# Ratio attention of a perceiver block: where GpSimd's value spread, key spread and bias addition stand against the tile's exponentials

## The chip, the cores and the metric

The kernel runs on one core of a Trainium2 chip. The time is the device time of one execution in microseconds; the kernel before has a median of 784.0 us over three runs, from 782.09 to 784.91. Smaller is better.

## The reference

Two layers run over x, 32 batches of 32 tokens with 256 features, each token's part added to x: a cross attention with a distance bias over 257 context rows, the **ratio attention**, a quantised feed-forward net, a second cross attention, a long and a segment attention, and a mixture of experts. The change touches the ratio attention alone:

```
qkv = layernorm(x) @ w_qkv + b_qkv;  q, k, v in 16 heads of 16
dot = q . k
vals = |q|^2 + |k|^2
scores = dot * dot / (vals - 2 dot + 1e-6) + causal mask (-1e9)
out = softmax(scores) @ v @ w_out + b_out;  x = x + out
```

## The kernel before, in words

The 1024 tokens are 8 tiles of 128 tokens (4 batches of 32). Five engines have instruction streams of their own and meet at semaphores only. The cross attention runs first, about to 260 us of the span, then the ratio attention to about 358 us, then the rest.

In the ratio attention each engine runs one step function per slot u, and one slot handles several tiles at different depths. The steps u = -2 (or -3) to 6 are in the block of the cross attention; what is left of tile 7 runs in the next block, after a barrier of all engines. The work of one tile n, in the order of its data:

- **Norm**: VectorE takes statistics (`norm_stats`, L1158 to L1163), GpSimd the inverse root (`root`, L1013 to L1015), VectorE applies it (`norm_apply`, L1169) in slot n - 4.
- **Projection**: TensorE turns the tile (L848), ScalarE copies it (L1074), TensorE projects queries and keys (L856), ScalarE evicts them (L1085 to L1093).
- **Key spread**: GpSimd multiplies the keys by head masks into `kbd` (helper `spread_heads`, L872, two instructions, slot n - 2). ScalarE squares `kbd` (L1078). TensorE forms numerator and denominator (helper `per_batch`, L896, slot n - 1).
- **Scores**: ScalarE evicts the denominator (L1102) and the squared numerator (L1104), VectorE takes the reciprocal (L1225), GpSimd multiplies (L1045) and adds the causal mask (L1048).
- **Softmax**, slot n: VectorE takes the row maximum (L1187) and subtracts it (L1188), ScalarE takes the exponentials (L1065, semaphore `p_ready`), VectorE turns blocks (helper `turn_blocks`, L933).
- **Values**: ScalarE copies the projected values (L1108), GpSimd spreads them by batch into `vbd` (helper `spread_batches`, L879, slot n). TensorE weighs them (helper `weigh_values`, L923). ScalarE takes sums and own heads (L1055, L1058), VectorE normalises and turns them (L1174, L1175, L956), TensorE projects (L865), VectorE adds the result to x (L1205). That last addition needs the output bias row in x already: GpSimd adds it (L1039, semaphore `bias_added`), in slot n - 2.

GpSimd's step u of the kernel before, in its queue's order: root of tile u+4, value spread of u, key spread of u+2, bias addition of u+2, multiplication and mask of u+1. VectorE's step u: statistics of u+4, normalising and turning of u-1, output addition of u-2, maximum and subtraction of u, `norm_apply` of u+4, block turning of u, reciprocal of u+1. The order is written out by hand in the step functions; nothing schedules it otherwise.

Of the kernel before, what the change touches and what calls it, by code (L numbers as in the profile page):

```python
# [21 lines left out]
ALU = mybir.AluOpType  # L22
# [44 lines left out]
def at_least(eng, sem, value):  # L67

    if isinstance(value, int) and value <= 0:
        return  # L70
    eng.wait_ge(sem, value)
# [797 lines left out]
def spread_heads(eng, kbd, kT, head):  # L869

    src = kT[:].rearrange("p (b k) -> p b k", b=BT)
    return eng.tensor_tensor(kbd, src.unsqueeze(2).broadcast_to([P, BT, 4, SQ]),  # L872
                             head.unsqueeze(1).unsqueeze(3).broadcast_to([P, BT, 4, SQ]), ALU.mult)


def spread_batches(eng, vbd, v, c):

    each = [P, 2 * NG, 2, 32]
    return eng.tensor_tensor(vbd[:, :, :, 0:32], v[:].rearrange("p (n d) -> p n d", d=32).unsqueeze(2).broadcast_to(each),  # L879
                             c.pair.unsqueeze(1).unsqueeze(3).broadcast_to(each), ALU.mult)  # L880
# [93 lines left out]
def there(u, count=NT):  # L974
    return not isinstance(u, int) or 0 <= u < count


class RatioAttention:


    def __init__(self, nc, sb, sem, psum, bank, c, x, w, loaded):
# [3 lines left out]
        bq2, wide, row = sb("bq2", [P, KT]), sb("wide", [P, KT, P]), sb("row", [P, D])  # L985
# [13 lines left out]
        consts_set, marked, row_full, row_ready = sem("consts_set"), sem("marked"), sem("row_full"), sem("row_ready")  # L999
        var_ready, rstd_ready, xn_ready = sem("var_ready"), sem("rstd_ready"), sem("xn_ready")  # L1000
# [5 lines left out]
        sub_ready, p_ready, pT_ready = sem("sub_ready"), sem("p_ready"), sem("pT_ready")  # L1006
        o_full, o_read, o_ready, oT_ready = sem("o_full"), sem("o_read"), sem("o_ready"), sem("oT_ready")
        y_full, y_done, bias_added = sem("y_full"), sem("y_done"), sem("bias_added")
# [4 lines left out]
        def root(pool, n):  # L1013
            pool.wait_ge(var_ready, n + 1)
            nc.gpsimd.tensor_tensor(rstd[n % 2][:], veps[n % 2][:], c.half[:, 0:1], ALU.pow).then_inc(rstd_ready, 1)  # L1015
# [5 lines left out]
            pool.wait_ge(marked, 2)  # L1021

        def pool_step(pool, u):
            if there(u + 4):
                root(pool, u + 4)
            if there(u):
                pool.wait_ge(v_done, u + 1)
                at_least(pool, o_full, u - 1)
                spread_batches(nc.gpsimd, vbd[u % 2], v, c).then_inc(vbd_ready, 1)
            if there(u + 2):  # L1030
                n = u + 2
                pool.wait_ge(k_ready, n + 1)
                at_least(pool, s_full, n - 1)
                for m in range(KT):
                    ins = spread_heads(nc.gpsimd, kbd[n % 2][:, m, :, :, :], kT[:, m, :], c.head)
                ins.then_inc(kbd_ready, 1)
                pool.wait_ge(xn_ready, n + 1)
                pool.wait_ge(row_ready, 1)
                nc.gpsimd.tensor_tensor(x[:, n, :], x[:, n, :], row[:], ALU.add).then_inc(bias_added, 1)  # L1039
            if there(u + 1):  # L1040
                n = u + 1
                pool.wait_ge(s_read, n + 1)
                pool.wait_ge(inverse_ready, n + 1)
                at_least(pool, p_ready, n - 1)
                nc.gpsimd.tensor_tensor(num[n % 2][:], square[n % 2][:], inverse[n % 2][:], ALU.mult) \  # L1045
                    .then_inc(ratio_ready, 1)
                pool.wait_ge(ratio_ready, n + 1)
                nc.gpsimd.tensor_tensor(num[n % 2][:], num[n % 2][:],  # L1048
                                        c.causal.unsqueeze(1).broadcast_to([P, NH, SQ]), ALU.add) \
                    .then_inc(masked_ready, 1)  # L1050

        def act_own(act, n):
            act.wait_ge(o_full, n + 1)
            at_least(act, o_ready, n)
            nc.scalar.copy(sums[:].rearrange("p (i b) -> p i b", b=BT), shares(o_banks)[:, :, :, 32])  # L1055
            for h in range(4):
                mine, at = slice(SQ * h, SQ * h + SQ), DH * (h % 2)
                ins = nc.scalar.copy(o_own[mine, :].rearrange("p (b i d) -> p i b d", b=BT, i=NG),  # L1058
                                     shares(o_banks)[mine, :, :, at:at + DH])
            ins.then_inc(o_read, 1)  # L1060
# [166 lines left out]
        self.root, self.norm_stats, self.norm_apply = root, norm_stats, norm_apply  # L1227
        self.pool_start, self.pe_start, self.dve_start, self.dve_row = pool_start, pe_start, dve_start, dve_row
        self.pool, self.act, self.pe, self.dve = pool_step, act_step, pe_step, dve_step
        self.act_own, self.act_exp, self.pe_output, self.pe_values = act_own, act_exp, pe_output, pe_values  # L1230
        self.dve_features, self.dve_output = features, dve_output
# [1703 lines left out]
```

## Time and profile before

| what | value |
|---|---|
| median of three runs | 784.0 us (782.09 to 784.91) |
| the profiled execution | 782.49 us, its span 780.7 us |
| TensorE busy | 659.7 us (84%), mean granted clock 0.938 |
| VectorE busy | 496.9 us (64%) |
| ScalarE busy | 359.7 us (46%) |
| GpSimd busy | 311.6 us (40%) |

The span is the time from the first to the last instruction seen by the profiler; 1.79 us of the execution lie around it. The shares are means over all stages. In the rows below PE is TensorE, PEld its weight load, DVE VectorE, ACT ScalarE, POOL GpSimd. PEclk is the granted clock as a share of 2.4 GHz. In the timeline a row is: start us, duration us, engine, line, operation, out<-in, count, and in brackets the idle time before it and what ended it. An instruction's duration includes time in which it has been issued and can't proceed. Buffer numbers are left out, and `late`, `shared` are regions in which the tiles of the ratio attention lie.

### The profile page before, as it was taken

To read this page: it belongs to the slowest core of one execution; us is meant where nothing else is said; L and a number is where in the kernel's file an instruction comes from. 1 tells how busy PE (TensorE), PEld (TensorE's weight loads), DVE (VectorE), ACT (ScalarE), POOL (GpSimd) and SP (SyncE) were. 2 spreads that over 40 slices of the span, in tenths; PEclk is the share of its full clock that TensorE was granted. 3 is DMA by queue.
4 is the path that set the end of the run, shared out by engine and by line. 5 is a ranking of instruction groups with operands and counts; after the bars stand their busy time and mean duration, and the time that the engine had idled before them with its cause. 6 is when DMAs were issued, how large, how long until landed. Compare 5 with 4: busy or idle time off the path is not lost. (4 is left out here: it accounts for less than half of the span.)

```text
span 780.7 us, 16875 instructions
## 1 busy us (share of the span) xinstructions
PE 659.7 (84%) x6081; PEld 502.5 (64%) x6081; DVE 496.9 (64%) x1365; ACT 359.7 (46%) x976; POOL 311.6 (40%) x445
## 2 busy tenths in 40 slices
PE   4999999999999877744993699978998884999990
PEld 3768777877877766643441587657776662677770
DVE  3677776776776789857368873556886786333330
ACT  1445454545545566734375753434655541223220
POOL 2244545555552377731000020233745533455641
PEclk9999999999999999976997799998999996999996
DMA  9632323222220000007500134609101021234334
GB/s 276 218 75 62 78 60 78 76 66 72 65 55 2 2 3 3 3 1 229 230 2 0 68 155 170 258 3 406 68 3 61 2 83 54 42 65 67 60 47 67
DMA packets 31697, 65.08 MB, mean 83 GB/s; under 512 B 5792, under 2 KB 21792, under 8 KB 29312
## 3 DMA queue, kind: packets, MB, share of 16 engines
q1 hardware_dynamic: 26016, 55.73, 21.7%
q0 software_dynamic: 4688, 7.18, 5.8%
q10 hardware_dynamic: 912, 1.10, 0.5%
q8 instruction: 50, 0.82, 0.4%
q14 instruction: 31, 0.25, 0.1%
HBM read 57.67 MB, written 7.37 MB: 83 GB/s over the span
## 5 line engine op out<-in xcount | busy, mean ns | idle before, releaser
L487 ACT ACTIVATE prob<-s_sb,negm 128x257 f32<-128x257 f32 x128 | 66.2, 517 | 94.2 <-DVE negm L710 94.2
L424 POOL TENSOR_SCALAR bias<-dist,cst 128x257 f32<-128x257 f32 x128 | 59.8, 486 | 97.8 <-DVE dist L697 88.0
L706 DVE CUSTOM_DVE_ANT_0 s_sb<-psum,bias 128x257 f32<-128x257 f32 x128 | 49.4, 423 | 51.5 <-PE psum L567 48.2
L545 PE MATMUL psum<-ctxT,shared 128*128 128x257 f32 x256 | 62.9, 389 | 1.7 <-DMA msk<-in_mask 1.7
L553 PE MATMUL psum<-shared,ctxT 128*128 128x256 f32 x256 | 60.4, 379 | 0.0
L2616 PE MATMUL psum<-ex_w,shared 128*128 x184 | 58.3, 460 | 0.6 <-ACT shared L2509 0.6
L1706 POOL TENSOR_TENSOR wn<-wn,cst 128x1 f32<-128x1 f32 x8 | 4.7, 588 | 123.9 <-DVE wn L1833 123.9
L553 PEld LDWEIGHTS psum<-shared,ctxT 128*128 128x128 f32 x256 | 48.4, 189 | 6.8
L545 PEld LDWEIGHTS psum<-ctxT,shared 128*128 128x128 f32 x256 | 47.2, 195 | 8.0 <-issue 2.4
L567 PE MATMUL psum<-kT,qbd 64*128 64x257 f32 x256 | 48.6, 429 | 2.7 <-DVE mx L706 2.5
L2616 PEld LDWEIGHTS psum<-ex_w,shared 128*128 128x128 f32 x184 | 33.1, 190 | 15.4 <-issue 0.8
L2800 DVE TENSOR_TENSOR shared<-psum,shared 128x352 f32<-128x352 f32 x23 | 12.1, 524 | 48.4 <-ACT shared L2525 48.4
L1445 PE MATMUL psum<-shared,ff_used_up 128*128 128x512 f32 x96 | 41.6, 593 | 0.0
L872 POOL TENSOR_TENSOR shared<-shared,cst 128x512 f32<-128x512 f32 x32 | 34.5, 1099 | 14.9 <-ACT shared L2038 14.9
L592 PE MATMUL psum<-pT,v 128*64 128x128 f32 x512 | 35.0, 279 | 2.8 <-DVE o_keys L759 2.8
L592 PEld LDWEIGHTS psum<-pT,v 128*64 128x64 f32 x512 | 27.4, 136 | 13.2 <-issue 13.1
L2525 ACT ACTIVATE shared<-psum 128x352 f32<-128x352 f32 x23 | 10.7, 464 | 52.8 <-PE psum L2616 52.8
L578 PE MATMUL psum<-cst,prob 128*128 128x128 f32 x256 | 35.0, 279 | 0.0
L2626 PE MATMUL psum<-ex_w,shared 128*128 x138 | 33.7, 380 | 0.8 <-DVE shared L2791 0.8
L567 PEld LDWEIGHTS psum<-kT,qbd 64*128 64x128 f32 x256 | 22.5, 184 | 18.4 <-DVE mx L706 10.0
L856 PE MATMUL psum<-shared,late 128*128 128x128 f32 x256 | 34.3, 290 | 0.0
L578 PEld LDWEIGHTS psum<-cst,prob 128*128 128x128 f32 x256 | 27.4, 141 | 10.5 <-issue 10.5
(349 smaller groups left out, 1656.5 us busy)
## 6 DMA issues: line engine op xcount, KB each, us to landing
ctxT<-in_ctx_T SPq DMA_DIRECT2D x32, 257.0 KB
ex_w<-in_w SPq DMA_DIRECT2D x1, 5632.0 KB, 17.3
kpos<-in_kpos SPq DMA_DIRECT2D x32, 128.5 KB
msk<-in_mask SPq DMA_DIRECT2D x32, 128.5 KB
near_turned<-in_ctx_T_tiles SPq DMA_DIRECT2D x4, 1028.0 KB
ff_used_up<-in_ctx_T_tiles SPq DMA_DIRECT2D x4, 1028.0 KB
near_rows<-in_ctx_tiles SPq DMA_DIRECT2D x4, 1024.0 KB, 7.5
ff_used_up<-in_ctx_tiles SPq DMA_DIRECT2D x4, 1024.0 KB, 7.2
```

Source lines behind the costliest of these rows:

```text
L424: nc.gpsimd.tensor_scalar(bias[n % 2][:, g, :], dist[n % 2][:], c.slope[:, g:g + 1], 1.0, ALU.mult, ALU.mult).then_inc(bias_ready, 1)
L487: nc.scalar.activation(prob[n % 2][:, g, :], s_sb[n % 2][:, g, :], ACT.Exp, bias=negm[:, b, g:g + 1], accum_out=esum[t % 2][:, b, g:g + 1]) \
L545: ins = nc.tensor.matmul(kv[m][:, 0:SK], w["xa_k"][:, k, P * m:P * m + P], ctxT[n % BT][:, k, :], start=(k == 0), stop=(k == KT - 1))
L553: ins = nc.tensor.matmul(kv[0][:, D * i:D * i + D], ctxT[n % BT][:, k, P * i:P * i + P], w["xa_v"][:, k, :], start=(i == 0 and k == 0), st ...
L567: nc.tensor.matmul(sc[g % 2][:, 0:SK], qbd[t % 2][lo:lo + 64, g // 2, b, :, :].rearrange("p h q -> p (h q)"), kT[n % 2][lo:lo + 64, g // 2 ...
L578: ins = nc.tensor.transpose(pt[j][:, at:at + P], prob[n % 2][:, g, P * i:P * i + P], c.ident)
L592: ins = nc.tensor.matmul(oo[64 * half:64 * half + 64, at:at + P], v[n % BT][:, i, 64 * g:64 * g + 64], pT[n % 2][:, g, i, :], start=(n % 2 ...
L706: nc.vector.tensor_tensor_reduce(s_sb[n % 2][:, g, :], sc[g % 2][:, 0:SK], bias[n % 2][:, g, :], 1.0, float("-inf"), ALU.add, ALU.max, mx[ ...
L856: ins = nc.tensor.matmul(dst[:, P * m:P * m + P], weight[:, k, P * m:P * m + P], xT[:, k, :], start=(m == 0 and k == 0), stop=True, skip_g ...
L872: return eng.tensor_tensor(kbd, src.unsqueeze(2).broadcast_to([P, BT, 4, SQ]), head.unsqueeze(1).unsqueeze(3).broadcast_to([P, BT, 4, SQ]) ...
L1445: ins = nc.tensor.matmul(bank[2 + n % 6][:], wt[:, k, P * m:P * m + P], xT[:, k, 512 * h:512 * h + 512], start=(k == 0), stop=(k == KT - 1))
L2616: ins = nc.tensor.matmul(y_bank[part][:, 0:FE], rT[j % 2][:, k, :], ex.w1[:, bass.ds(e, 1), k, FE * part:FE * part + FE].rearrange("p a f ...
```

## The change

In GpSimd's step the bias addition is moved ahead of the value spread and gets one wait more: for the exponentials of tile u, where u is 0 or more. As the queue is in order, value spread and key spread stand behind that wait too. The root moves from the head of step u (tile u+4) to the end of step u (tile u+5), and the first root, of tile 2, is called at the head of step -2. Nothing else changes: the operations, their number and their operands are the same.

```diff
         def pool_step(pool, u):
-            if there(u + 4):
-                root(pool, u + 4)
+            if u == -2:
+                root(pool, 2)
+            if there(u + 2):
+                n = u + 2
+                pool.wait_ge(xn_ready, n + 1)
+                pool.wait_ge(row_ready, 1)
+                at_least(pool, p_ready, u + 1)
+                nc.gpsimd.tensor_tensor(x[:, n, :], x[:, n, :], row[:], ALU.add).then_inc(bias_added, 1)
             if there(u):
                 pool.wait_ge(v_done, u + 1)
                 at_least(pool, o_full, u - 1)
@@ -1034,9 +1040,6 @@
                 for m in range(KT):
                     ins = spread_heads(nc.gpsimd, kbd[n % 2][:, m, :, :, :], kT[:, m, :], c.head)
                 ins.then_inc(kbd_ready, 1)
-                pool.wait_ge(xn_ready, n + 1)
-                pool.wait_ge(row_ready, 1)
-                nc.gpsimd.tensor_tensor(x[:, n, :], x[:, n, :], row[:], ALU.add).then_inc(bias_added, 1)
             if there(u + 1):
                 n = u + 1
                 pool.wait_ge(s_read, n + 1)
@@ -1048,6 +1051,8 @@
                 nc.gpsimd.tensor_tensor(num[n % 2][:], num[n % 2][:],
                                         c.causal.unsqueeze(1).broadcast_to([P, NH, SQ]), ALU.add) \
                     .then_inc(masked_ready, 1)
+            if there(u + 5):
+                root(pool, u + 5)
```

`at_least` issues no wait for a value of zero or less, and `there(n)` is true for tiles 0 to 7.

## Rows read from the trace of the kernel before

**Rows 1.** Page, busy time by engine: us, share of the span, instructions.
```profile
PE 659.7 (84%) x6081; PEld 502.5 (64%) x6081; DVE 496.9 (64%) x1365; ACT 359.7 (46%) x976; POOL 311.6 (40%) x445
```

**Rows 2.** Windows, the slot of tile 2: length, busy PE, PEld, DVE, ACT, POOL, PEclk, DMA.
```profile
296.50:306.30 9.80, 6.92 (x175) 6.18 (x181) 9.23 (x13) 6.47 (x17) 7.23 (x8) 0.83 0.00 0
```

**Rows 3.** Timeline, VectorE, tile 2's maximum up to tile 3's.
```profile
296.50 0.69 DVE L1187 TENSOR_REDUCE shared<-late 128x16 f32<-128x512 f32 x1 [0.37 <-POOL late L1048]
297.22 1.31 DVE L1188 TENSOR_TENSOR late<-late,shared 128x512 f32<-128x512 f32 x1
298.45 1.13 DVE L1169 TENSOR_SCALAR shared<-x,shared 128x256 f32<-128x256 f32 x1
299.50 0.70 DVE L933 STREAM_TRANSPOSE late<-late 128x512 f32<-128x512 f32 x1
300.13 3.30 DVE L1225 RECIPROCAL late<-late 128x512 f32<-128x512 f32 x1
...
304.32 0.79 DVE L1175 TENSOR_TENSOR shared<-shared 128x256 f32<-128x256 f32 x1
...
306.29 0.69 DVE L1187 TENSOR_REDUCE shared<-late 128x16 f32<-128x512 f32 x1 [0.39 <-POOL late L1048]
```

**Rows 4.** Timeline, GpSimd, the same slot.
```profile
296.43 0.55 POOL L1015 TENSOR_TENSOR shared<-shared,cst 128x1 f32<-128x1 f32 x1
296.94 1.04 POOL L879 TENSOR_TENSOR shared<-shared,cst 128x512 f32<-128x512 f32 x1
297.94 2.54 POOL L872 TENSOR_TENSOR late<-shared,cst 128x512 f32<-128x512 f32 x2
300.44 0.63 POOL L1039 TENSOR_TENSOR x<-x,shared 128x256 f32<-128x256 f32 x1
303.56 1.27 POOL L1045 TENSOR_TENSOR late<-late 128x512 f32<-128x512 f32 x1 [2.50 <-issue]
304.91 1.35 POOL L1048 TENSOR_TENSOR late<-late,cst 128x512 f32<-128x512 f32 x1
```

**Rows 5.** Timeline, GpSimd, the key spread of tile 0, before the slots.
```profile
263.88 2.04 POOL L872 TENSOR_TENSOR late<-shared,cst 128x512 f32<-128x512 f32 x2 [3.31 <-ACT shared L1085]
```

**Rows 6.** Timeline, VectorE, tile 4's slot, and tile 7's subtraction after it.
```profile
316.09 0.69 DVE L1187 TENSOR_REDUCE shared<-late 128x16 f32<-128x512 f32 x1 [0.37 <-POOL late L1048]
316.81 0.79 DVE L1188 TENSOR_TENSOR late<-late,shared 128x512 f32<-128x512 f32 x1
318.30 0.71 DVE L933 STREAM_TRANSPOSE late<-late 128x512 f32<-128x512 f32 x1 [0.70 <-ACT late L1065]
...
325.10 0.69 DVE L1187 TENSOR_REDUCE shared<-late 128x16 f32<-128x512 f32 x1 [0.37 <-POOL late L1048]
...
348.18 0.69 DVE L1188 TENSOR_TENSOR late<-late,shared 128x512 f32<-128x512 f32 x1
```

**Rows 7.** Source view of `norm_apply`: ns min/median/max, first and last start us.
```profile
L1169 DVE TENSOR_SCALAR shared<-x,shared x8: 415/1126/1129, 234.6 to 308.2; 128x256 f32<-128x256 f32 x8
```

**Rows 8.** Timeline, ScalarE: value copy, own heads, and tile 4's exponentials.
```profile
300.15 0.37 ACT L1108 COPY shared<-psum 128x256 f32<-128x256 f32 x1
...
301.09 1.50 ACT L1058 COPY shared<-psum 32x256 f32<-32x256 f32 x4
...
317.64 0.63 ACT L1065 ACTIVATE late<-late 128x512 f32<-128x512 f32 x1 [2.36 <-DVE late L1188]
```

**Rows 9.** Timeline, TensorE: tile 2's slot, and two rows of tile 7's scores.
```profile
300.25 0.70 PE L923 MATMUL psum<-shared,late 64*64 64x66 f32 x32 [2.88 <-DVE late L933]
...
301.16 3.12 PE L856 MATMUL psum<-shared 128*128 128x128 f32 x16
...
305.97 0.70 PE L896 MATMUL psum<-shared,cst 64*32 64x128 f32 x32
...
328.70 1.75 PE L896 MATMUL psum<-late,shared 64*32 64x128 f32 x64
...
331.54 1.06 PE L896 MATMUL psum<-shared,cst 64*32 64x128 f32 x32 [0.24 <-ACT shared L1078]
```

## The prediction

> **What bounds the kernel now.** The page first: TensorE is busy 84% of the span and GpSimd 40% [rows 1]. That is a mean over stages and says nothing of this one. The windows by slot show another picture: in tile 2's slot of 9.80 us VectorE is busy 9.23, GpSimd 7.23 and TensorE 6.92 us, although TensorE's granted clock is 0.83 there [rows 2]. So the timelines of VectorE and GpSimd decide. A slot runs from one tile's row maximum to the next's. In tile 2's slot VectorE goes maximum 296.50, subtraction 297.22, `norm_apply` 298.45, block turning 299.50, reciprocal 300.13 [rows 3]; GpSimd goes on with the multiplication at 303.56 and the mask at 304.91, and the next maximum starts at 306.29 [rows 3, 4]. It is one loop through two engines with no gap: 9.79 us. Four slots have this form, of tiles 0 to 3; from tile 4 on there is no `norm_apply` left and a slot is 325.10 - 316.09 = 9.01 us [rows 6].
>
> Two instructions in that loop are longer than their work. The subtraction takes 1.31 us [rows 3], and 0.69 when GpSimd is idle [rows 6]. `norm_apply` takes 1.13 us, and its shortest record is 0.415 [rows 3, 7]. GpSimd's rows say why: the value spread ends at 297.98, and the subtraction, issued at 297.22, ends 0.55 us after that; `norm_apply`, issued at 298.45, ends at 299.58, after the first of the two key spreads, which are 2.54 us together here and 2.04 where nothing collides [rows 4, 5]. Whichever of the two engines comes second stands until the other's instruction is over. In tile 4's slot, with no root ahead of it, the value spread comes earlier and the subtraction needs 0.79 [rows 6].
>
> The Trainium skill has this rule, on the page "SBUF — State Buffer", section "SBUF: two separate sides": GpSimd and VectorE share a port pair that is held for a whole instruction, and VectorE wants it with two SBUF inputs or in a two-port mode. The trace agrees for the subtraction, at 1.31 against 0.69 us. Was the reciprocal to want the pair too, the change would lose: the bias addition would stand until the reciprocal is over, and the slot would come to some 12 us. Rows exclude it: the bias addition ran at 300.44 for 0.63 us inside the reciprocal of 300.13 to 303.43, and the second key spread lay beside the block turning, which took 0.70 us, as against 0.71 in tile 4's slot [rows 3, 4, 6].
>
> **The change, part by part.** It adds and removes no instruction but the wait.
>
> *Root.* In the queue's cyclic order it stays between the mask of one tile and the spreads of the next; called at the end of a step, it is only kept ahead of the new wait. It runs from 0.07 us ahead of the maximum to 0.48 behind its start [rows 3, 4], and the subtraction starts at +0.72: no collision. Cost 0.
>
> *Wait for the exponentials.* It stands in the steps of tiles 0 to 5; in tile 6's the bias addition, and the wait with it, doesn't exist, so that slot stays as it is. Let 0 be the start of the maximum. The subtraction starts at +0.72 and now takes 0.69 us. In tile 4's slot the exponentials start at +1.55 [rows 6, 8] with 0.10 us of collision in it (0.79 less 0.69), so they start at +1.45 and end at +2.08. `norm_apply` runs behind the subtraction from about +1.34 to +1.75, beside the exponentials and with GpSimd idle: hidden, with 0.3 us to spare. Block turning: +2.21 in tile 4's slot [rows 6], less 0.10: +2.11. It was +3.00 [rows 3]. From there on the loop is as it was: 0.63 to the reciprocal, 3.43 to the multiplication (+6.17), 1.35 to the mask, 1.38 to the next maximum: 8.90 us. So 4 slots give 0.89 us each, 3.56, and tiles 4 and 5 give 0.10 each, 0.20. Sum 3.76 us.
>
> *What is queued behind the wait.* GpSimd starts at +2.15 (0.07 behind the exponentials) with 0.63 for the bias, 1.04 for the value spread and 2.04 for the key spread [rows 4, 5]: 3.71, so it is done at +5.86, and the multiplication is wanted at +6.17. Cover 0.31 us. Beside it VectorE only turns blocks and takes the reciprocal, which do not collide (above). If the key spread stayed at 2.54, GpSimd would be 0.19 late in 6 slots and give back 1.1 us.
>
> *Who waits for the spreads.* The value spread of the tile now ends at +3.82 instead of +1.48. The weighing of values on TensorE starts at +3.75 now [rows 3, 9] and would start at +3.9. ScalarE's copy of the next tile's values, at +3.65 now [rows 8], waits for the same spread, so it goes to about +3.85 and ends at +4.2; the own heads behind it start 0.84 us after the weighing [rows 8, 9], at +4.7, and end at +6.2. VectorE wants them only after its reciprocal at +6.05, ahead of a normalisation that must stand for the multiplication anyway (0.79 us at 304.32 [rows 3]). Hidden. TensorE: after the values at 300.25 the last part of the scores ended at 306.67, 6.42 us later, with the slow clock in between [rows 9]; from +3.9 that is +10.3. Those scores are evicted behind the next exponentials, at 8.90 + 2.0 = +10.9. Cover 0.6 us in a slot like this. The key spread, at +5.86, is ahead of the squares (after the own heads, at +6.5) and of the scores. So all of it costs 0, and what is late next is TensorE.
>
> *Before and after the slots.* In step -2 the bias addition moves into idle time (3.31 us ahead of the first key spread [rows 5]); in step -1 it delays a key spread by 0.63 us, which no loop needs then. After tile 6 a barrier follows GpSimd's last mask; all behind it, loads included, is released by semaphores of this stage and moves up as a whole. 0.
>
> The sum against the profiled execution: 782.49 - 3.76 = 778.7 us. That execution lies 1.5 us under the median of 784.0, so on the median's footing it is 780.2, a ratio of 0.9952. About 0.3%, or 2.35 us, is what a measurement of this kernel can tell from no change.
>
> **The rivals.**
>
> *Less of the gain.* The wait is longer than the 0.07 us I take from ScalarE to GpSimd, or the spreads take their collided length. Each 0.1 us beyond the cover of 0.31 costs 0.6 us. With 0.5 us late in each of 6 slots, 3.0 of 3.76 are given back: 783.2. For: it is a cover of 0.3 us in a loop with three engines. Against: every duration in it is from a row. Chance 0.13.
>
> *TensorE becomes the bound* (the other side). Its granted clock falls to 1.2 GHz in some slots: the projection takes 3.12 us in tile 2's slot, and tile 7's scores, slow throughout, ran from 328.70 to 332.60, 3.9 us, against 2.4 here (from the end of the projection, 304.28, to 306.67) [rows 9]. Slow throughout, the scores would end 0.91 + 3.12 + 3.9 = 7.9 us after the values began, at +11.8 or later with the turning slow too (+12.1). It decides once they end behind +10.9. A slot would be 8.90 + 1.2 = 10.1 us, six of them 60.6 against 57.2 now (4 of 9.79 and 2 of 9.01): 3.4 slower, 787.4. For: the values begin no earlier in a slot that is shorter. Against: the slow stretches cover part of a slot only (0.83 in the mean [rows 2]), and shorter slots leave TensorE less idle time. Chance 0.05.
>
> The skill's page "TensorE: Matmul & The Clock Gate", section "What's actually happening", ties the clock to how busy the array has been lately; by it the shorter slots speak against this rival. No row here shows a slot of 8.9 us.
>
> *No change to speak of.* The stage gets shorter, but what follows takes it back: a barrier, a load or a slow clock behind the ratio attention that doesn't move with it. Nothing there waits for an absolute time. 784.0. Chance 0.10.
>
> **How the numbers follow.** Forecast 0.72, the rivals 0.13, 0.05 and 0.10. The predicted time is the likeliest's, 780.2. The range: the runs of before spread from 1.9 under to 0.9 over their median; a luckier clock takes it to 778.0, and upward it takes in the smaller gains and stops at 783.8 (about 0.1 lies above, 0.08 below). Faster by over 0.3%: 0.72 less the part that noise hides plus the milder half of the first rival, 0.71; same 0.23; slower 0.06.
>
> **What would show it right or wrong.** Right: subtraction at 0.69, `norm_apply` at 0.42, the key spread pair at 2.04 us; slots of 8.9 us for tiles 0 to 5; GpSimd idle ahead of the bias addition, released by L1065, and 0.3 us idle ahead of the multiplication. Wrong: a multiplication with no idle time ahead of it (GpSimd late), an eviction at L1102 that waits for L896 (TensorE), a subtraction still over 1 us (the collision was not with the spreads), or a block turning that waits for anything but the exponentials.

## The result, and the profile after

| | before | changed |
|---|---|---|
| median of 12 runs | 783.56 us (781.96 to 785.27) | 780.39 us (778.25 to 782.14) |
| profiled execution | 782.49 us, span 780.7 | 778.49 us, span 776.7 |
| mean granted clock of TensorE | 0.938 | 0.940 |
| VectorE busy | 496.9 us | 490.4 us |
| GpSimd busy | 311.6 us | 309.6 us |

The ratio is 0.996, with a 95% interval of 0.9946 to 0.9974: 3.1 us gained, between 2.0 and 4.2. The changed kernel is faster by 0.4%, beyond the 0.3% that can be told from no change, though the interval's near end, 0.26%, is just inside it. The lines of the helpers (L872, L879, L896, L923, L933, L956) keep their numbers; `norm_apply` is L1174 now (was L1169), the maximum L1192 (L1187), the subtraction L1193 (L1188), the reciprocal L1230 (L1225), the normalisation L1180 (L1175), the bias addition L1031 (L1039), multiplication and mask L1048 and L1051 (L1045, L1048), the exponentials L1070 (L1065), the value copy L1113 (L1108).

First the timeline of VectorE in the changed kernel, tile 2's slot and then tile 4's, as in [rows 3] and [rows 6]:

```profile
294.92 0.69 DVE L1192 TENSOR_REDUCE shared<-late 128x16 f32<-128x512 f32 x1 [0.39 <-POOL late L1051]
295.64 0.69 DVE L1193 TENSOR_TENSOR late<-late,shared 128x512 f32<-128x512 f32 x1
296.25 0.41 DVE L1174 TENSOR_SCALAR shared<-x,shared 128x256 f32<-128x256 f32 x1
297.02 0.71 DVE L933 STREAM_TRANSPOSE late<-late 128x512 f32<-128x512 f32 x1 [0.37 <-ACT late L1070]
297.66 3.31 DVE L1230 RECIPROCAL late<-late 128x512 f32<-128x512 f32 x1
...
303.85 0.69 DVE L1192 TENSOR_REDUCE shared<-late 128x16 f32<-128x512 f32 x1 [0.39 <-POOL late L1051]
...
312.75 0.69 DVE L1192 TENSOR_REDUCE shared<-late 128x16 f32<-128x512 f32 x1 [0.38 <-POOL late L1051]
313.47 0.69 DVE L1193 TENSOR_TENSOR late<-late,shared 128x512 f32<-128x512 f32 x1
...
321.67 0.69 DVE L1192 TENSOR_REDUCE shared<-late 128x16 f32<-128x512 f32 x1 [0.38 <-POOL late L1051]
```

The subtraction is down from 1.31 to 0.69 us, `norm_apply` from 1.13 to 0.41. The block turning starts 2.10 us after the maximum (3.00 before) and stands 0.37 us for the exponentials: the chain through ScalarE is now what VectorE waits for there. Tile 2's slot takes 303.85 - 294.92 = 8.93 us, tile 4's 8.92.

GpSimd in the same slot, as in [rows 4]:

```profile
294.84 0.55 POOL L1015 TENSOR_TENSOR shared<-shared,cst 128x1 f32<-128x1 f32 x1
297.16 0.64 POOL L1031 TENSOR_TENSOR x<-x,shared 128x256 f32<-128x256 f32 x1 [1.77 <-ACT late L1070]
297.75 1.04 POOL L879 TENSOR_TENSOR shared<-shared,cst 128x512 f32<-128x512 f32 x1
298.75 2.04 POOL L872 TENSOR_TENSOR late<-shared,cst 128x512 f32<-128x512 f32 x2
301.10 1.28 POOL L1048 TENSOR_TENSOR late<-late 128x512 f32<-128x512 f32 x1 [0.31 <-issue]
302.46 1.35 POOL L1051 TENSOR_TENSOR late<-late,cst 128x512 f32<-128x512 f32 x1
```

It idles for 1.77 us while the subtraction and `norm_apply` run, then does its three jobs at full speed (the key spread pair takes 2.04 us, not 2.54), and is done 0.31 us before the multiplication. Before the change the idle time stood ahead of the multiplication, 2.50 us in one piece [rows 4].

Where the 4.0 us of the two profiled spans went: tile 0's maximum starts at 277.06 (276.90 before) and tile 6's at 330.60 (334.10), so the six slots between them take 53.54 us instead of 57.20: **3.66 us less**. Behind them the first matmul of the feed-forward net (L1445, now L1450) starts at 366.4 instead of 370.1, and the first of the experts (L2616, now L2621) at 659.0 instead of 662.9. What was won in the stage is carried to the end.

### The profile page after: what moved, and what is told of

It is laid out like the page before. It is cut to its first block and busy times, and to the rows that moved or that the text cites. A ratio compares the mean times of both kernels' runs of the same rounds, so it can differ in the third digit from the quotient of the medians.

```text
span 776.7 us, 16875 instructions
## 1 busy us (share of the span) xinstructions
PE 656.7 (85%) x6081; PEld 501.0 (64%) x6081; DVE 490.4 (63%) x1365; ACT 360.6 (46%) x976; POOL 309.6 (40%) x445
## 5 line engine op out<-in xcount | busy, mean ns | idle before, releaser
L2621 PE MATMUL psum<-ex_w,shared 128*128 x184 | 58.3, 460 | 0.6 <-ACT shared L2514 0.6
L2621 PEld LDWEIGHTS psum<-ex_w,shared 128*128 128x128 f32 x184 | 33.1, 190 | 15.4 <-issue 0.8
L1450 PE MATMUL psum<-shared,ff_used_up 128*128 128x512 f32 x96 | 41.6, 593 | 0.0
L872 POOL TENSOR_TENSOR shared<-shared,cst 128x512 f32<-128x512 f32 x32 | 34.5, 1100 | 14.9 <-ACT shared L2043 14.9
```

The costliest lines, as they stand in the source:

```text
L1450: ins = nc.tensor.matmul(bank[2 + n % 6][:], wt[:, k, P * m:P * m + P], xT[:, k, 512 * h:512 * h + 512], start=(k == 0), stop=(k == KT - 1))
L2621: ins = nc.tensor.matmul(y_bank[part][:, 0:FE], rT[j % 2][:, k, :], ex.w1[:, bass.ds(e, 1), k, FE * part:FE * part + FE].rearrange("p a f ...
```

## The experiments

Three questions: is it the collision on the port, or the order of GpSimd's queue, that gave the gain; how much room does GpSimd have behind the wait; and what would use the idle time better. The port theory is that of the prediction. Its rival, the order theory, is that the bias addition no longer stands last ahead of the multiplication, and that this shortens the slot. The first four kernels ran on one chip and the last four on another, each beside the kernel before, so kernels of the two groups are compared by their ratios to it. Slots are read from the starts of the maxima. An edit moves the line numbers behind it by a few lines.

**The changed kernel again.** No edit.

> The changed kernel once more, as the mate of the others on this chip. Expected 3.2 to 3.8 us under the kernel before, ratio about 0.9955: slots of tiles 0 to 5 at 8.92 us, subtraction 0.69, norm_apply 0.41, key spread pair 2.04.

780.77 us, ratio 0.9959 (0.9946 to 0.9972). The slots of tiles 0 to 5 take 53.54 us again, 276.89 to 330.43.

**Without the wait.**

```diff
                 pool.wait_ge(row_ready, 1)
-                at_least(pool, p_ready, u + 1)
                 nc.gpsimd.tensor_tensor(x[:, n, :], x[:, n, :], row[:], ALU.add).then_inc(bias_added, 1)
```

> The changed order (bias addition first, root at the end) without the wait for the exponentials. Port theory: the bias addition runs from +0.48 to +1.1 after the maximum's start, the subtraction stands for it and ends at about +1.7, the value spread follows and norm_apply stands for it; block turning at about +3.0 as in the kernel before, slots of tiles 0 to 3 at 9.7 to 9.9 us, time 783.5, ratio 0.999 to 1.002. Order theory (the gain comes from the bias addition no longer standing last, ahead of the multiplication, and the wait adds nothing): slots of 8.9 us, ratio about 0.996.

784.06 us, ratio 1.0004 (0.9991 to 1.0018): nothing is left of the gain. The timelines of VectorE (tile 2's slot, then tile 4's) and of GpSimd beside them:

```profile
295.53 0.69 DVE L1191 TENSOR_REDUCE shared<-late 128x16 f32<-128x512 f32 x1 [0.38 <-POOL late L1050]
296.25 0.90 DVE L1192 TENSOR_TENSOR late<-late,shared 128x512 f32<-128x512 f32 x1
297.08 1.12 DVE L1173 TENSOR_SCALAR shared<-x,shared 128x256 f32<-128x256 f32 x1
298.13 0.70 DVE L933 STREAM_TRANSPOSE late<-late 128x512 f32<-128x512 f32 x1
...
304.92 0.69 DVE L1191 TENSOR_REDUCE shared<-late 128x16 f32<-128x512 f32 x1 [0.37 <-POOL late L1050]
...
315.06 1.38 DVE L1192 TENSOR_TENSOR late<-late,shared 128x512 f32<-128x512 f32 x1
```

```profile
295.98 0.63 POOL L1030 TENSOR_TENSOR x<-x,shared 128x256 f32<-128x256 f32 x1
296.57 1.49 POOL L879 TENSOR_TENSOR shared<-shared,cst 128x512 f32<-128x512 f32 x1
...
314.84 1.05 POOL L879 TENSOR_TENSOR shared<-shared,cst 128x512 f32<-128x512 f32 x1
```

The collisions are back with the wait gone, with other partners: the subtraction stands for the shorter bias addition (0.90 us), `norm_apply` for the value spread (1.12). So the slots of tiles 0 to 3 are 9.39 to 9.41 us, not the 9.7 to 9.9 that I expected, and those of tiles 4 and 5, where there is no root to push the spreads back, are 9.60 and 9.59, longer than before (9.01 and 9.00): there the value spread starts at 314.84, the subtraction is issued at 315.06 and takes 1.38 us. The six slots sum to 56.78 us against 57.20. The order theory, with its slots of 8.9, is out; the new order alone trades one collision for another.

**Waiting for the subtraction instead of the exponentials.**

```diff
-                at_least(pool, p_ready, u + 1)
+                at_least(pool, sub_ready, u + 1)
```

> The wait is for the subtraction of the tile instead of its exponentials. Port theory: norm_apply is issued at +1.34, ahead of the bias addition at about +1.5, so it has the port first and takes 0.41; the bias addition stands for it some 0.3 us; slots stay at 8.92 us, GpSimd is idle 0.8 us or so ahead of the multiplication instead of 0.31, the time is that of the changed kernel within 0.3 us. Rival (whoever is awake first takes the port, and norm_apply loses it): norm_apply 1.0 us, block turning at +2.4, four slots longer by 0.3 us, 1.2 us slower than the changed kernel.

780.25 us, ratio 0.9948 (0.993 to 0.9966). In the timelines of VectorE and GpSimd:

```profile
296.12 0.41 DVE L1174 TENSOR_SCALAR shared<-x,shared 128x256 f32<-128x256 f32 x1
296.90 0.71 DVE L933 STREAM_TRANSPOSE late<-late 128x512 f32<-128x512 f32 x1 [0.37 <-ACT late L1070]
```

```profile
296.38 0.65 POOL L1031 TENSOR_TENSOR x<-x,shared 128x256 f32<-128x256 f32 x1 [1.11 <-DVE late L1193]
...
300.98 1.29 POOL L1048 TENSOR_TENSOR late<-late 128x512 f32<-128x512 f32 x1 [0.95 <-issue]
```

The bias addition is issued 0.26 us after `norm_apply` and leaves it alone: 0.41 us. One part of the expectation failed: the bias addition was to stand some 0.3 us for `norm_apply`, and it takes 0.65 us, against 0.64 with no collision. When it is issued, 0.15 us of `norm_apply` are left (to 296.53). The subtraction's rows show the same allowance: its stall is shorter by 0.14 to 0.15 us than what is left of GpSimd's instruction when it is issued (left 0.76, stalled 0.62 in [rows 3, 4]; 0.36 and 0.21, then 0.83 and 0.69, in the kernel without the wait). So a rest of 0.15 us costs next to nothing; why isn't shown. Slots stay at 8.91 to 8.93 us, with 0.95 us of room ahead of the multiplication instead of 0.31. The wait need not be for the exponentials. It is enough that it keeps GpSimd off until the last VectorE instruction that wants the port is under way. Its eight runs go from 777.7 to 781.3 us, the three shortest at a mean granted clock of 0.936 to 0.940 and the other five at 0.927 to 0.933. The interval doesn't place this kernel ahead of the changed one.

**The value spread ahead of the wait.** The block of `spread_batches` stands first in the step, then wait and bias addition, then the key spread.

> The value spread runs ahead of the wait, as in the kernel before; bias addition and key spread behind it. Port theory: the subtraction collides with the value spread (1.31 us in the slots of tiles 0 to 3, 0.79 in those of 4 and 5), norm_apply does not (0.41); block turning at +2.73, slots of tiles 0 to 3 at 9.5 us and of 4 and 5 at 9.0, time 1.1 us under the kernel before, ratio 0.9986. Order theory: as the changed kernel, ratio 0.996, as the same instructions stand ahead of the multiplication.

782.74 us, ratio 0.9994 (0.9981 to 1.0007). The interval doesn't tell this from no change. The trace tells more (VectorE, tile 2's slot):

```profile
296.30 0.69 DVE L1192 TENSOR_REDUCE shared<-late 128x16 f32<-128x512 f32 x1 [0.37 <-POOL late L1051]
297.02 1.31 DVE L1193 TENSOR_TENSOR late<-late,shared 128x512 f32<-128x512 f32 x1
298.25 0.40 DVE L1174 TENSOR_SCALAR shared<-x,shared 128x256 f32<-128x256 f32 x1
299.02 0.71 DVE L933 STREAM_TRANSPOSE late<-late 128x512 f32<-128x512 f32 x1 [0.37 <-ACT late L1070]
...
305.84 0.69 DVE L1192 TENSOR_REDUCE shared<-late 128x16 f32<-128x512 f32 x1 [0.39 <-POOL late L1051]
```

One collision is back (1.31 us), the other is not (0.40). The slots are 9.53 to 9.55 us and 9.01, as expected to 0.05. This splits the 0.87 us per slot: 0.61 from the subtraction, 0.26 from `norm_apply`. The second is less than the 0.72 us by which that instruction got shorter, because from there on the exponentials end last.

**The bias addition back behind the spreads,** the wait kept, ahead of the value spread.

```diff
             if there(u + 2):
-                n = u + 2
-                pool.wait_ge(xn_ready, n + 1)
-                pool.wait_ge(row_ready, 1)
                 at_least(pool, p_ready, u + 1)
-                nc.gpsimd.tensor_tensor(x[:, n, :], x[:, n, :], row[:], ALU.add).then_inc(bias_added, 1)
             if there(u):
...
                 ins.then_inc(kbd_ready, 1)
+                pool.wait_ge(xn_ready, n + 1)
+                pool.wait_ge(row_ready, 1)
+                nc.gpsimd.tensor_tensor(x[:, n, :], x[:, n, :], row[:], ALU.add).then_inc(bias_added, 1)
```

> The wait for the exponentials stays, ahead of the value spread; the bias addition goes back behind the two spreads. Port theory: slots of 8.92 us, GpSimd idle 0.31 us ahead of the multiplication, time that of the changed kernel within noise, ratio 0.996; the values are weighed 0.6 us earlier and nothing gains from it. Order theory (the place of the bias addition has a share in the gain): slots longer than 8.92 us, by up to 0.6.

780.35 us, ratio 0.9956 (0.9942 to 0.997), slots of 8.91 to 8.93 us, with 0.40 us idle ahead of the multiplication where I expected 0.31. The place of the bias addition is worth nothing. Nor is the root's: the end of one step and the head of the next are the same place in the queue, so each tile's root is called where it was, ahead of the wait. So GpSimd's instructions here are in the order of the kernel before, with the wait as the one addition, and the wait alone carries the gain.

**One more key spread instruction behind the wait,** in the steps of tiles 0 to 5.

```diff
+                if there(u):
+                    spread_heads(nc.gpsimd, kbd[n % 2][:, 0, :, :, :], kT[:, 0, :], c.head).then_inc(padded, 1)
+                    pool.wait_ge(padded, u + 1)
                 for m in range(KT):
```

> The first key spread instruction is done once more in the steps of tiles 0 to 5, with a wait on itself: 1.04 us and about 0.07 more for GpSimd between the wait and the multiplication. If the cover is the 0.31 us of the trace, the multiplication comes 0.8 us late in 6 slots: slots of 9.7 us, 4.8 us slower than the changed kernel, ratio to the kernel before 1.002. If GpSimd had a full microsecond of room, slots stay at 8.92.

786.0 us, ratio 1.0038 (1.0021 to 1.0055), 5.6 us over the changed kernel's 780.4. GpSimd in one slot:

```profile
298.46 0.64 POOL L1032 TENSOR_TENSOR x<-x,shared 128x256 f32<-128x256 f32 x1 [1.77 <-ACT late L1074]
299.05 1.04 POOL L879 TENSOR_TENSOR shared<-shared,cst 128x512 f32<-128x512 f32 x1
300.05 3.16 POOL L872 TENSOR_TENSOR late<-shared,cst 128x512 f32<-128x512 f32 x3
303.17 1.27 POOL L1052 TENSOR_TENSOR late<-late 128x512 f32<-128x512 f32 x1
```

There is no idle time ahead of the multiplication any more, and the six slots take 58.44 us (276.85 to 335.29), 4.90 more than in the changed kernel: 0.82 each in the mean for 1.12 us of added work. The last three are the longer ones (9.79 to 9.81 us against 9.67 to 9.70): there the multiplication, now later, takes 1.46 or 1.47 us instead of 1.28, issued while a normalisation of VectorE runs. The rest of the 5.6 us isn't in the slots and was not followed up. The room was 0.3 us, as the idle time said; a microsecond more on GpSimd makes the kernel slower than it was before the change.

**Reciprocal, multiplication and mask in halves,** with the wait for the exponentials, and then with the wait for the subtraction. ScalarE's wait on `ratio_ready` counts two for a tile.

```diff
-                pool.wait_ge(inverse_ready, n + 1)
...
-                nc.gpsimd.tensor_tensor(num[n % 2][:], square[n % 2][:], inverse[n % 2][:], ALU.mult) \
-                    .then_inc(ratio_ready, 1)
...
+                for h in range(2):
+                    at = slice(8 * h, 8 * h + 8)
+                    pool.wait_ge(inverse_ready, 2 * n + h + 1)
+                    nc.gpsimd.tensor_tensor(num[n % 2][:, at, :], square[n % 2][:, at, :], inverse[n % 2][:, at, :],
+                                            ALU.mult).then_inc(ratio_ready, 1)
+                    pool.wait_ge(ratio_ready, 2 * n + h + 1)
+                    ins = nc.gpsimd.tensor_tensor(num[n % 2][:, at, :], num[n % 2][:, at, :],
+                                                  c.causal.unsqueeze(1).broadcast_to([P, NH // 2, SQ]), ALU.add)
...
-                nc.vector.reciprocal(inverse[n % 2][:], inverse[n % 2][:]).then_inc(inverse_ready, 1)
+                for h in range(2):
+                    half = inverse[n % 2][:, 8 * h:8 * h + 8, :]
+                    nc.vector.reciprocal(half, half).then_inc(inverse_ready, 1)
```

> The changed kernel with reciprocal, multiplication and mask in two halves of 8 heads each, so that GpSimd's first half can run beside VectorE's second. With the wait for the exponentials GpSimd is done with the spreads at +5.86 only, so it is the bound: four instructions of 0.65 to 0.7 us from there, mask ends at +8.6: slots of 8.65 us, 0.27 less in 6 slots, and tile 7's mask some 1.2 us earlier as there nothing keeps GpSimd: 2.8 us under the changed kernel, ratio to before 0.992.

781.38 us, ratio 0.9974 (0.9963 to 0.9985): no better than the changed kernel, where I expected 2.8 us less. GpSimd in a slot, and VectorE's normalisation beside it:

```profile
298.24 2.04 POOL L872 TENSOR_TENSOR late<-shared,cst 128x512 f32<-128x512 f32 x2
300.24 0.72 POOL L1050 TENSOR_TENSOR late<-late 128x256 f32<-128x256 f32 x1
301.04 0.73 POOL L1053 TENSOR_TENSOR late<-late,cst 128x256 f32<-128x256 f32 x1
301.73 0.91 POOL L1050 TENSOR_TENSOR late<-late 128x256 f32<-128x256 f32 x1
302.71 0.73 POOL L1053 TENSOR_TENSOR late<-late,cst 128x256 f32<-128x256 f32 x1
303.41 0.55 POOL L1015 TENSOR_TENSOR shared<-shared,cst 128x1 f32<-128x1 f32 x1
```

```profile
301.36 0.69 DVE L1182 TENSOR_TENSOR shared<-shared 128x256 f32<-128x256 f32 x1
```

GpSimd is the bound here, as expected, but the four halves take 3.17 us (300.24 to 303.41) where the two whole ones take 2.66 (301.10 to 303.76 in the changed kernel): a half costs 0.72 us, not 0.65, each mask starts 0.08 us behind its multiplication, and one of the four is longer: the second multiplication takes 0.91 us, issued while the normalisation runs (301.36 to 302.05). The expectation had counted no collision there. The slots are 9.11 us in the mean (276.24 to 330.90). Tile 7, whose multiplication GpSimd awaits idle, does gain: its mask ends 7.89 us after tile 6's maximum, against 9.01. The 1.12 us gained there and the 1.12 us lost in the six slots (54.66 against 53.54) cancel.

> The same with the wait for the subtraction in place of the exponentials: GpSimd is free at +5.25, first half done by +6.6, second half by +8.0 to +8.3 with VectorE's normalisation standing for the port in between: slots of 8.4 us, 0.5 less in 6 slots and 1.2 at tile 7: 4.2 us under the changed kernel, ratio to before 0.990. If VectorE (8.4 us busy in a slot of 8.9) is the bound instead, the maximum will have no idle time ahead of it and slots stay above 8.6.

**776.08 us, ratio 0.9909 (0.9888 to 0.993)**, faster than both kernels. The wait is the only difference from the kernel above. The end of tile 2's slot on VectorE, its output addition and the next maximum:

```profile
301.21 0.39 DVE L1212 TENSOR_TENSOR x<-psum,x 128x256 f32<-128x256 f32 x1
301.52 0.67 DVE L1194 TENSOR_REDUCE shared<-late 128x16 f32<-128x512 f32 x1
```

The six slots take 50.42 us (276.39 to 326.81), 8.40 each, as expected, and tile 7 gains as above. In the slots of tiles 0 to 2 VectorE has no idle time left ahead of the next maximum (the bracket that the other kernels show is missing), so there VectorE has become the bound, and what is left to take is mostly its 0.37 us ahead of the block turning. I had expected slots above 8.6 us in that case, from 8.4 us of work on VectorE in a slot; it is 8.00 in the changed kernel's windows below, and the slots are no longer than where GpSimd is the bound. From tile 3's slot on, with fewer norms to take, it waits 0.65 us for the mask again.

## Why the prediction was right

780.2 us was forecast, 780.4 was measured, and the parts agree. That the two times lie so close is in part luck: the forecast took 3.8 us off a median of 784.0 over three runs, and over twelve that median is 783.56 and the gain 3.1 us, its interval up to 4.2. What bears the forecast out is the trace:

- **The term that carries it.** 0.89 us per slot for tiles 0 to 3 was 0.87, 0.87, 0.86 and 0.90; 0.10 for tiles 4 and 5 was 0.09 and 0.07. The sum is 3.66 against 3.76 us. The block turning came at +2.10, and the multiplication at +6.18 (+2.11 and +6.17 predicted).
- **The cover behind the wait.** Predicted 0.31 us, measured 0.31, but by two errors that cancel. The bias addition starts at +2.24, not +2.15: it comes 0.17 us behind the exponentials (which end at 296.99), not 0.07. And from there to the end of the key spread it is 3.63 us, not 3.71, since the rows of instructions that follow each other overlap by 0.04 or 0.05 us. The added key spread made the cover show: this was the first rival's condition, and its price per 0.1 us holds (0.81 us beyond the cover, six times, is 4.9 us, and 4.90 was measured). The spreads didn't keep their collided length.
- **The page's rule.** "SBUF — State Buffer", section "SBUF: two separate sides", in the Trainium skill says that the port pair is held by one engine for a whole instruction. The subtraction agrees at 0.69, 0.90, 1.31 and 1.38 us, according to what GpSimd had begun before it, with the allowance of 0.14 to 0.15 us that is told above, and the reciprocal at 3.31 us beside three spreads. I had weighed, and ruled out by rows, that the reciprocal wants the pair too; the trace after agrees.
- **The place of the bias addition and of the root.** Costed at nothing, and the run with the bias addition last shows both, as told there.
- **TensorE, the other side.** It never decided: in tile 2's slot its clock was 1.00, and in tile 3's 0.81, and both slots took 8.9 us. Two of the six slots were at 0.81, as against three below 0.84 before. But the cover is as thin as I had put it, 0.6 us: in tile 3's slot the last scores end at 314.22 and their eviction starts at 314.73, 0.5 us later. The rival's sum for a slow clock throughout was too mild: it took 3.12 us for the projection, a row that is slow in part only, against 1.95 at the full clock. The windows by slot of the changed kernel, columns as in [rows 2], and those two instructions in its timeline:

```profile
294.92:303.85 8.93, 6.74 (x187) 5.82 (x187) 8.00 (x13) 6.49 (x19) 6.78 (x8) 1.00 0.02 5
303.85:312.75 8.90, 6.71 (x98) 5.94 (x105) 7.43 (x10) 5.66 (x15) 6.71 (x7) 0.81 0.01 2
```

```profile
299.80 1.95 PE L856 MATMUL psum<-shared 128*128 128x128 f32 x16
...
313.52 0.70 PE L896 MATMUL psum<-shared,cst 64*32 64x128 f32 x32
...
314.73 0.67 ACT L1107 ACTIVATE late<-psum,shared 128x512 f32<-128x512 f32 x1
```

Three details were off without moving the time. The key spread isn't ahead of the scores everywhere, as I had put it: in the last of the six steps TensorE has no projection to do and waits 1.25 us for it. The timelines of TensorE and ScalarE in the changed kernel:

```profile
325.65 0.70 PE L923 MATMUL psum<-shared,late 64*64 64x66 f32 x32 [2.22 <-issue]
327.60 1.16 PE L896 MATMUL psum<-late,shared 64*32 64x128 f32 x64 [1.25 <-POOL late L872]
```

```profile
298.88 0.38 ACT L1113 COPY shared<-psum 128x256 f32<-128x256 f32 x1 [0.83 <-POOL shared L879]
...
332.80 0.69 ACT L1107 ACTIVATE late<-psum,shared 128x512 f32<-128x512 f32 x1
```

Those scores are evicted at 332.80, three microseconds after they end, so it is covered. The value copy on ScalarE stands 0.83 us for the value spread, and comes at +3.96 rather than +3.85. And VectorE stands for the own heads, 0.62 us in the slot of tile 3, where I had them in time; the normalisation behind them (0.78 us, from 310.80) stands for the multiplication (310.03 to 311.30) anyway.

Of the 4.0 us between the two profiled executions 3.66 are the six slots. The rest is smaller than the spread of either kernel's runs and was not followed up.

## What to carry to other kernels

Where an instruction on VectorE is longer in a slot than its shortest record, look at what GpSimd had begun when it was issued: the stall is about the rest of that instruction, and it is worth a wait on the other engine if the work so held back has idle time later in the loop. Such a wait costs nothing up to the idle time that the profile shows ahead of the held engine's next turn, here 0.3 us, and, in the run with the added key spread, everything beyond it. So let it end as early as the port allows, with VectorE's last colliding instruction issued, which is what left room for a further gain.

## What the runs showed of the hardware that I had not expected

Cutting a GpSimd instruction of 512 elements per partition in two gives 0.72 us for each half against 1.28 for the whole, and a wait of GpSimd on its own last instruction adds 0.08. Issue order by a fraction of a microsecond decides who stands: a bias addition issued 0.26 us behind `norm_apply` didn't lengthen it (0.41 us), and one issued 0.27 us ahead of the subtraction made it 0.90 instead of 0.69.
